# Order tables of all eight attention iterations and of the steps between the expert tiles rewritten

## The reference

```python
x = x + _L0_xattn_ref(_layernorm(x), ctx_768, ...)   # 8 heads of 64, softmax over 512 context tokens
x = x + _L0_ffn_ref(_layernorm(x), ...)              # 128->512->128, fixed point, piecewise linear Gelu
x = x + _L1_xattn_ref(_layernorm(x), ctx_768, ...)   # 16 heads of 8, then 128->256->128 with relu
x = x + _L1_ffn_ref(_layernorm(x), ...)              # 8 experts 128->512->128, top 2 of each token
```

## Time and profile before

| | us |
|---|---|
| median of 3 runs | 435.76 (434.94 to 436.88) |
| profiled execution, first to last instruction (span) | 435.2 |
| PE busy in it | 374.0 (86%) |
| DVE busy | 313.7 (72%) |
| ACT busy | 241.5 (55%) |
| POOL busy | 190.5 (44%) |

### The profile page before, as it was taken

The page is one execution under the profiler, slowest core; times in us unless marked ns, Lnnn a source line. Parts: engine busy times, 40 slices in busy tenths (PEclk is TensorE's granted clock), DMA queues, the critical chain, the costliest instruction groups (busy, mean ns, idle before and its releaser), DMA issues.

```text
span 435.2 us, 8264 instructions
## 1 busy us (share of the span) xinstructions
PE 374.0 (86%) x2779; PEld 209.4 (48%) x2779; DVE 313.7 (72%) x661; ACT 241.5 (55%) x473; POOL 190.5 (44%) x255
## 2 busy tenths in 40 slices
PE   7767799999789968988888979997999789999990
PEld 3413454675456526544532433343234466677660
DVE  7765775756776797777788678888964487677765
ACT  2703465655925462547557567775587534556551
POOL 5084635817355672554054604577150004206661
PEclk9956999999989988998699689999799999999997
DMA  7581818109204501032024300532013001511113
GB/s 190 114 196 46 180 30 183 36 2 200 56 1 109 149 0 36 2 98 75 26 57 125 97 26 28 182 96 74 12 34 97 2 14 49 139 30 50 50 50 96
DMA packets 46104, 33.02 MB, mean 76 GB/s; under 512 B 5952, under 2 KB 42944, under 8 KB 46064
## 3 DMA queue, kind: packets, MB, share of 16 engines
q1 hardware_dynamic: 44816, 29.93, 27.6%
q0 software_dynamic: 1248, 2.57, 1.9%
HBM read 15.13 MB, written 7.89 MB: 53 GB/s over the span
## 4 chain that ended last, share of the span: by engine, by line
PE 62%; DVE 18%; ACT 8%; issue 5%; DMA 3%; SPq 2%; POOL 0%; POOLq 0%; DVEq 0%; ACTq 0%
PE p_o L677 7%; DVE mx L938 7%; PE p_sc L643 6%; PE p_misc L537 5%; PE p_o L690 5%; PE p_misc L839 4%; PE p_sc L839 4%; PE p_sc L657 3%; PE p_misc L858 3%; ACT probs L1287 3%; PE p_o L850 3%; PE p_misc L603 3%; PE p_misc L563 2%; PE p_misc L732 2%; PE p_misc L722 2%
## 5 line engine op out<-in xcount | busy, mean ns | idle before, releaser
L938 DVE TENSOR_REDUCE mx<-p_misc 128x1 f32<-128x512 f32 x192 | 120.1, 683 | 25.4 <-PE p_misc L603 14.0
L1287 ACT ACTIVATE probs<-p_sc 128x512 f32<-128x512 f32 x128 | 69.4, 594 | 35.8 <-PE p_sc L657 34.5
L1295 ACT ACTIVATE probs<-p_sc 128x512 f32<-128x512 f32 x64 | 35.1, 598 | 30.0 <-PE p_sc L643 29.8
L1450 POOL TENSOR_TENSOR psums<-probs 128x256 f32<-128x256 f32 x32 | 24.1, 754 | 47.7 <-PE p_o L684 45.2
L1409 POOL TENSOR_SCALAR veps<-meanvar 128x2 f32<-128x2 f32 x16 | 3.8, 236 | 92.6 <-DVE meanvar L893 92.3
L690 PE MATMUL p_o<-probs,v 128*32 128x256 f32 x512 | 42.3, 412 | 1.2 <-ACT probs L1287 1.2
L657 PE MATMUL p_sc<-qS,kS 64*128 64x256 f16 x256 | 33.3, 285 | 6.6 <-ACT probs L1287 4.4
L677 PE MATMUL p_o<-probs,v 128*64 128x256 f32 x256 | 35.7, 400 | 3.7 <-ACT probs L1295 3.7
L643 PE MATMUL p_sc<-region 128*128 128x256 f16 x256 | 35.1, 282 | 2.0 <-DVE region L954 1.1
L1182 DVE TENSOR_TENSOR probs<-probs,p_sc 128x512 f32<-128x512 f32 x30 | 20.6, 686 | 22.5 <-ACT probs L1373 22.3
L1373 ACT ACTIVATE probs<-p_misc 128x512 f32<-128x512 f32 x30 | 17.9, 598 | 31.1 <-PE p_sc L839 31.1
(11 more groups left out here) (222 smaller groups left out, 757.9 us busy)
## 6 DMA issues: line engine op xcount, KB each, us to landing
region<-kx SPq DMA_DIRECT2D x24, 256.0 KB, 3.9
v<-in_L_ffn_W_dram SPq DMA_DIRECT2D x24, 256.0 KB, 2.7
region<-qx SPq DMA_DIRECT2D x24, 128.0 KB, 3.9
kS<-k_scratch SPq DMA_DIRECT2D x8, 192.0 KB
k_scratch<-kx SPq DMA_DIRECT2D x4, 256.0 KB, 2.6
slots_in<-none SPq DMA_DIRECT2D x1, 975.0 KB, 9.7
slots_in<-none SPq DMA_DIRECT2D x1, 960.0 KB, 5.4
slots_out<-probs SPq DMA_DIRECT2D x15, 64.0 KB, 1.6
```

The lines of the kernel that those rows point to most:

```text
L938: dve.tensor_reduce(mx[:, b % 2, i, head:head + 1], ps, AX_X, ALU.max).then_inc(free, 1)
L1287: act.activation(probs[:, (h + j) % 8, half * 512:(half + 1) * 512], p_sc[:, j, :], ACT.Exp, scale=DH1 ** -0.5).then_inc(sc_free[j], 1)
L1295: act.activation(probs[:, h % 8, half * 512:(half + 1) * 512], p_sc[:, half, :], ACT.Exp, scale=DH0 ** -0.5).then_inc(sc_free[half], 1)
```

## The change

All numbers of `SHIFTED` and of `REST` are replaced. The set of 714 steps and what each of them issues, waits for and allocates stay the same. One line of each table:

```diff
-    (3, 'up0'): (1.55, 0.05), (3, 'v0'): (-0.02, 0.71), (3, 'v1'): 4.95, (3, 'wipe'): -1.24,
+    (3, 'v0'): (-58.44, 0.64), (3, 'v1'): 3.73, (3, 'wipe'): 6.77, (3, 'y0'): (6.77, 0.53), (3, 'zeros'): -54.36,
...
-REST = [(0.0, 'oT1', 3, 0), (0.0, 'oT1', 3, 1), (1.31, 'aT1', 3), (1.4, 'numbers'), (1.81, 'h1', 3),
+    (0, 'oT1', 3, 0), (0, 'oT1', 3, 1), (0.55, 'aT1', 3), (0, 'numbers'), (1.17, 'h1', 3), (1.81, 'y1', 3),
```

Where the order is tested at the end of `schedule()`, a second chain is added:

```diff
     for b in range(B):
+        turn = [("sT", b), ("oT", b, 0), ("aT", b, 0), ("oT", b, 1), ("aT", b, 1)]
+        at = [order.index(what) for what in turn]
+        assert at == sorted(at), turn
```

More of the change, by code:

```diff
@@ L61 @@
 SHIFTED = {
[L62 to L66, removed]
@@ L85 @@
[L85 to L89, removed]
@@ L95 @@
[L95 to L99, removed]
@@ L130 @@
[L130 to L140 removed]
+    (0, 'aT'): (-25.39, 3.65), (0, 'av'): (-0.45, 0.55), (0, 'bounce'): -44.42, (0, 'down0'): -72.64,
@@ new lines @@
+    (3, 'f_xn'): -1.56, (3, 'floor'): 2.08, (3, 'ident'): 3.36, (3, 'init'): (6.82, 3.53), (3, 'interp'): 3.08,
[3 rows of a table added]
+    (3, 'sT'): 3.01, (3, 'slope'): 2.68, (3, 'stack'): -77.05, (3, 'sum'): 1.96, (3, 'up0'): (1.46, 0.05),
+    (3, 'v0'): (-58.44, 0.64), (3, 'v1'): 3.73, (3, 'wipe'): 6.77, (3, 'y0'): (6.77, 0.53), (3, 'zeros'): -54.36,
+    (4, 'aT'): (5.51, 2.11), (4, 'aT1'): -53.6, (4, 'av'): (-0.1, 0.87), (4, 'best'): 46.51, (4, 'bounce'): 12.08,
+    (4, 'compare'): 22.89, (4, 'consts'): -43.98, (4, 'count'): 57.13, (4, 'down0'): 7.79,
@@ new lines @@
+    (4, 'rank'): 12.13, (4, 'round'): 3.66, (4, 'route'): 55.59, (4, 'rows'): 2.34, (4, 'sT'): 3.76,
+    (4, 'send'): 98.07, (4, 'shares'): 2.11, (4, 'slope'): 5.07, (4, 'split'): (0.84, 2.16), (4, 'stack'): -7.18,
+    (4, 'stage'): (1.17, 1.77), (4, 'up0'): (2.09, 0.32), (4, 'v1'): 3.89, (4, 'weights'): 24.63,
+    (4, 'y0'): (6.19, 2.44), (4, 'y1'): -42.3, (5, 'aT'): (-29.55, 1.95), (5, 'aT1'): 5.17, (5, 'av'): (0.26, 1.16),
+    (5, 'best'): 60.09, (5, 'bounce'): 10.59, (5, 'compare'): -5.35, (5, 'consts'): -24.75, (5, 'count'): 9.75,
@@ new lines @@
+    (5, 'down0'): 7.93, (5, 'ex_ln'): (-0.38, 0.75), (5, 'ex_xT'): (80.15, 0.64), (5, 'ex_xn'): (-47.0, 1.73),
+    (5, 'f_ln'): -44.0, (5, 'f_xT'): 1.84, (5, 'f_xn'): -1.31, (5, 'fetch'): 3.34, (5, 'floor'): 3.28,
+    (5, 'gT'): (-3.9, 1.6), (5, 'h1'): 8.2, (5, 'ident'): 6.22, (5, 'interp'): 6.12, (5, 'k1'): 7.86,
+    (5, 'logits'): (-26.74, 1.32), (5, 'max'): (2.36, 1.15), (5, 'nodes'): 4.55, (5, 'oT'): (3.15, 0.87),
+    (5, 'oT1'): (3.39, 0.05), (5, 'place'): 81.48, (5, 'q1'): 12.41, (5, 'q1_ln'): 8.88, (5, 'q1_xT'): 11.62,
@@ new lines @@
+    (6, 'count'): 14.71, (6, 'down0'): -6.08, (6, 'ex_ln'): (7.2, 1.73), (6, 'ex_xT'): (10.16, 1.54),
+    (6, 'ex_xn'): (10.0, 0.56), (6, 'f_ln'): 8.48, (6, 'f_xT'): -29.46, (6, 'f_xn'): -0.97, (6, 'fetch'): 28.32,
+    (6, 'floor'): 18.59, (6, 'gT'): (29.86, 0.1), (6, 'h1'): 7.46, (6, 'ident'): 7.73, (6, 'interp'): -26.37,
+    (6, 'k1'): 67.09, (6, 'logits'): (11.48, 1.29), (6, 'max'): (3.6, 1.26), (6, 'nodes'): -19.71,
+    (6, 'oT'): (-41.13, 4.29), (6, 'oT1'): (4.08, 0.79), (6, 'place'): 13.96, (6, 'q1'): -10.94, (6, 'q1_ln'): 20.96,
@@ new lines @@
+    (7, 'consts'): 62.76, (7, 'count'): 41.96, (7, 'down0'): 56.12, (7, 'ex_ln'): (11.26, 0.65),
+    (7, 'ex_xT'): (16.29, 1.08), (7, 'ex_xn'): (13.86, 1.2), (7, 'f_ln'): 8.84, (7, 'f_xT'): -39.4,
+    (7, 'f_xn'): -20.79, (7, 'fetch'): 39.74, (7, 'floor'): 3.85, (7, 'gT'): (-16.01, 2.26), (7, 'h1'): 8.4,
+    (7, 'ident'): 9.91, (7, 'interp'): 22.8, (7, 'k1'): 38.98, (7, 'logits'): (29.75, 0.48),
+    (7, 'max'): (-24.94, 3.18), (7, 'nodes'): 0.46, (7, 'oT'): (4.15, 5.44), (7, 'oT1'): (3.58, 0.05),
```

94 lines of the change are left out of this document (40 added, 54 removed), and 17 rows, old and new, of the table SHIFTED.

## The result

| | before | after |
|---|---|---|
| median of 4 runs, us | 435.55 (434.94 to 436.88) | 455.77 (450.42 to 456.29) |
| profiled execution, span, us | 435.2 | 454.3 |
| mean granted clock in it | 0.930 | 0.910 |

The ratio is 1.043 (95% interval 1.038 to 1.048); the medians alone give 1.046, since one of the four executions took 450.4 us. In all times and ratios from here on, an execution more than 1.5% above the fastest of its kernel is left out. The forecast was 432.4, its range ended at 440.

What follows compares the result with a forecast made beforehand. PE was taken as the bound, busy 374.0 of 435.2 us. Terms -1.0 - 1.5 - 1.5 + 3.6 - 3.0 + 0 = -3.4 us gave a span of 431.8; with 0.56 for the median, 432.4, range 426.5 to 440.

Steps and rivals of the forecast that it cites:

- Start: First attention's start: v0 of batch 1 moves ahead of the first score step; -1.0 us (from -3 to +2).
- Feed-forward of batch 0: Behind up0: two more PE steps cover the Gelu hole of 1.59 us, perhaps no low clock in down0; -1.5 us.
- Feed-forward of batch 1: Four maxima instead of eight ahead of slope, Gelus earlier, the hole of 3.71 us shorter; -1.5 us (from -4 to +1.5).
- Fills: SP's queue, ahead of batch 1's stack1: kS lands 8.3 us later, PE stands about 5; +3.6 us (from 0 to +10).
- a price of the rival's size: Rival at the fills: they cost their full price, 10 to 12 us, nothing absorbed; time 440, chance 0.17.
- Routing: Batches 0 and 1: av and v1 steps close the logits' 2.02 us hole and the low clock behind it; -3.0 us.
- the holes only move: Rival, whole kernel: a filled hole opens at the next place, perhaps 2.5 of 7.0 us remain; time 437, chance 0.2.
- Expert tiles: Expert tiles: aT1 ahead of gu 1 costs 0.8 us, dn 1 wins 0.8; sum 0 (from -1 to +1.5).
- the sign that it is wrong: Wrong if the first score step's lateness isn't regained by batch 1's first score, or new holes stand where PE was full.
- Rest of the second attention: Second attention beyond the fills: costs nothing, within 1 us, since bounce and stack1 keep their places for batches 2 and 3.

Runs made afterwards that it cites:

- the old table: The changed kernel with the whole table of the expert tiles as before: 446.2 us, 1.024 to the kernel before.
- the fills first: The changed kernel with the two fills alone put ahead of batch 1's bounce: 448.9 us, 1.028 to the kernel before.
- the fetch later: The changed kernel with the second fetch alone two expert tiles later: 443.9 us, 1.020 to the kernel before.
- two losses undone: The changed kernel with the fills ahead of batch 1's bounce and the old table of the expert tiles: 443.2 us, 1.015 to the kernel before.
- those of iterations 0 to 5: The change's numbers put into the kernel before: iterations 0 to 2, 438.0 us; 3 (early fills), 442.1; 4 and 5, 443.9; 0 to 5 (early fills), 443.8.

## Why the prediction was wrong, by its steps

- **Start, -1.0.** The cost was right: `v0` takes 5.32 us (5.5 were worked out) and the first score step is 3.4 us later (about 3). The gain was not: +0.1 by batch 2 instead of -1.0. The step held everything else in the stretch of batch 1 fixed. Its PE work fell by only 1.9 us (32.13 to 30.25), since eight matmuls of `max` came in where `v0` and an `av` step left, and PE was idle there for 1.35 us instead of 0.17.
- **Feed-forward of batch 0, -1.5.** The -1.1 of the two profiled executions agrees by luck. The step took the low clock in `down0` for a part of the order, and it was one execution's: with the old order nine of ten others take 40.1 us from batch 2's first score to batch 3's, the trace of before 41.6, the new order 40.5. The hole of 1.59 us was filled, but `down0` starts 1.5 us later (23.5 against 22.0 us behind batch 2's first score; about 1 was allowed for), and no gain is left. The start and this part alone cost 2 us.
- **Feed-forward of batch 1, -1.5.** Failed, with the wrong sign: +4.7 in the profiled execution. The step counted four maxima fewer ahead of `slope`, and by that `slope` does come 1.3 us earlier where the clock holds, about half of the 2.4 forecast. In the profiled execution it started at 159.57 instead of 159.00, because `up0` ran at half clock (3.75 us instead of 1.97) and DVE waited for the Gelus behind it. What the step didn't look at is PE's own waits. `xn` now stands right behind the statistics and waits 1.40 us for POOL's `rstd` (it ends at 144.22 us), where a `max` lay between them, and `xT` stands ahead of a score step on PE, so PE waits 1.90 us for it and `up0` starts 1.4 us later behind batch 3's first score. And the reads that free PE's banks stand behind `slope` on DVE: the hole of 3.71 became two of 1.82 and 2.30. In other executions of this order PE loses 1.5 us here (the old table; the fills first) or 4.7 (the fetch later; two losses undone), put in alone 3.4 and 5 us of the time.
- **Fills, +3.6.** Right: a hole of 4.01 us where 5 were forecast. From the first score of the second attention to that of its batch 1 the changed kernel loses 1.8 us and the one with early fills wins 1.3, so 3.1 are the fills'; in the time it is 6.9 us with the new table of the expert tiles and 3.0 with the old (446.2 against 443.2). The low clock stood in the range and not in the sum: behind the hole PE ran at 0.50 from 206 to 212 us. In the kernel before, where PE comes to the place earlier, a price of the rival's size was paid (10 us).
- **Routing, -3.0.** Failed: +3.3 from score 8 of batch 2 to the first tile in the profile, +1.4 or nothing when put in alone. The step counted three more `av` and `v1` ahead of the logits, 2.7 us. From score 8 of batch 2 to the logits PE has one `av` step more (32 matmuls instead of 24) and `v1`, 1.5 us by the same prices. And it took the hole's length and the low clock behind it as won once work is put in front. Part of that work is missing behind it, DVE sets the pace, and the clock fell all the same. This is the rival "the holes only move".
- **Expert tiles, 0.** The step that failed most: +9.0. It looked at `aT1` and `dn` 1, at places where PE had holes before, and put the rest at nothing, though the prediction itself says that an order can make holes where PE is full, and names such holes as the sign that it is wrong. It looked past `numbers` (4 us alone), and past the order of `place`, `send` and `fetch` against the stores (4 us alone; undoing the fetch gave about 10 in the changed kernel). That order is on SP and POOL and had slack in the trace of before. The order of SP was read for the fills and not here.
- **Rest of the second attention, 0 within 1.** +1.3.

In sum the feed-forward of batch 1, the routing and the expert tiles miss by 6.2, 6.3 and 9.0 us in the profiled execution, and the rest together by 1.0: 22.5 us, from the forecast span of 431.8 to 454.3. The sum is exact because it compares two executions; each term carries their clocks. The parts put in one at a time don't add up as exactly, since each mixture has its own seams: those of iterations 0 to 5 cost 2, 5 and 8 us, and 6 together. Which order within iterations 4 and 5 makes their 8 us, beyond the wait for `qS`, stays open.

## What to carry to other kernels

When a table moves everything, go by queues and not by holes: for each engine that only issues (SP, POOL) list what each blocking wait holds up behind it, and how much slack the buffers behind it have, above all where PE was full before. Here an early fetch cost PE 0.8 us by itself, and 5 to 6.6 us when the scatters that it waits for moved the other way as well. In the routing, filling a hole with work from behind it won nothing, since the next engine set the pace there. And before a low clock in one trace is priced as a gain, look at a second execution of the same order: the one in `down0` was gone in most of them.

## What was not expected of the hardware

- The same order of instructions ran at different clocks in different executions. The changed kernel's profile, and then that of the run with the old table of the expert tiles, whose order up to there is the same:

```profile
149.00:152.00 3.00, 3.00 (x8) 2.17 (x7) 1.32 (x3) 0.84 (x2) 0.02 (x1) 0.50 0.00 0
```

```profile
149.00:152.00 3.00, 3.00 (x23) 1.49 (x21) 1.67 (x3) 2.26 (x6) 0.00 (x0) 1.00 0.02 5
```

  PE ran this stretch behind the same hole of 1.90 us, in front of `xT` of batch 1, in both. About 3 us of the +4.7 above are this. The runs of one kernel lie up to 7 us apart (before, over all comparisons: 432.6 to 440.0).
- A hole of 0.81 us, in the stretch of the logits, was followed by half clock as well as one of 2.02, and one of 1.59 us, in front of `down0`, in two of eleven executions. The run with `numbers` alone moved, with its hole of 2.46 us and the half clock behind it, cost 4.3 us.
